# Softmax sums of an attention block: four buffers of P, other blocks summed by GpSimd, query and key roundings on ScalarE

## The reference

```python
def attention(x, Wq, bq, Wk, bk, Wv, bv, Wp, bp):
    q, k, v = heads(x @ Wq + bq), heads(x @ Wk + bk), heads(x @ Wv + bv)
    att = jnp.einsum('bhtd,bhsd->bhts', q, k) * (1.0 / math.sqrt(D))
    # mask: causal, and every fourth key (s % 4 == 3) is left out
    att = jax.nn.softmax(jnp.where(mask == 0, -jnp.inf, att), axis=-1)
    y = jnp.einsum('bhts,bhsd->bhtd', att, v)
    return merge_heads(y) @ Wp + bp

x = x + _layernorm(attention(_layernorm(x), ...))
idx = jnp.argmax(jax.nn.log_softmax(logits) - jnp.log(-jnp.log(u)))
x = x + _layernorm(_layernorm(x) @ W[idx] + b[idx])
```

## Time and profile before

| | |
|---|---|
| median of 3 runs | 2435.17 us (2433.01 to 2436.12) |
| the profiled execution | 2434.55 us |
| its span, first to last instruction | 2432.6 us |
| mean granted TensorE clock | 0.987 of full speed |
| busy: PE / ACT / DVE / POOL | 2321.4 / 1719.4 / 1686.6 / 1408.3 us |

### The profile page before, as it was taken

One profiled execution on the slowest core, in us unless ns is written; L12 is line 12 of the kernel. 1 busy time (PEld: TensorE's weight loads), 2 busy tenths in 40 slices (PEclk: granted clock), 3 DMA queues, 4 the chain that ended last, 5 costly groups with the idle time before them and its releaser, 6 DMA issues.

```text
span 2432.6 us, 43804 instructions
## 1 busy us (share of the span) xinstructions
PE 2321.4 (95%) x15380; PEld 966.1 (40%) x15380; DVE 1686.6 (69%) x4832; ACT 1719.4 (71%) x3142; POOL 1408.3 (58%) x1318
## 2 busy tenths in 40 slices
PE   4899999999999999999999999999899999999996
PEld 2444443433454443433344443343334444334322
DVE  7867677676477678677466867777728676777774
ACT  6667676777777667677776867767767676776673
POOL 2245465685655457477854637657765455665734
PEclk9899999999999999999999999999999999999998
DMA  7213131121233113022132313102114231301001
GB/s 197 67 42 93 28 78 35 41 55 41 50 89 78 57 43 80 17 51 51 33 87 59 92 31 75 48 23 58 38 46 94 60 80 31 83 22 40 30 1 35
DMA packets 224357, 137.50 MB, mean 57 GB/s; under 512 B 146730, under 2 KB 196618, under 8 KB 224138
## 3 DMA queue, kind: packets, MB, share of 16 engines
q1 hardware_dynamic: 222310, 134.65, 22.1%
q10 hardware_dynamic: 1828, 0.07, 0.1%
HBM read 39.69 MB, written 16.78 MB: 23 GB/s over the span
## 4 chain that ended last, share of the span: by engine, by line
PE 74%; DVE 10%; ACT 6%; issue 5%; POOL 5%; DMA 1%; SPq 0%; POOLq 0%; ACTq 0%; DVEq 0%
PE acc L1303 13%; PE acc L1267 12%; PE acc L1287 11%; PE acc L1238 9%; PE acc L1239 9%; PE acc L1240 9%; PE acc L1318 8%; ACT P L949 4%; POOL P L817 3%; DVE acc L1042 2%; PE acc L1291 2%; DVE MP L1046 2%; DVE MHL L1057 1%; PE acc L1243 1%; DVE STA L1015 1%
## 5 line engine op out<-in xcount | busy, mean ns | idle before, releaser
L949 ACT ACTIVATE P<-acc,EX 128x512 f32<-128x512 f32 (+2 forms) x1920 | 1073.1, 641 | 314.5 <-PE acc L1291 153.9
L1046 DVE TENSOR_REDUCE MP<-acc 128x1 f32<-128x512 f32 (+1 forms) x1088 | 720.6, 679 | 254.2 <-PE acc L1267 250.7
L817 POOL TENSOR_TENSOR P<-P 128x512 f32<-128x512 f32 x546 | 682.3, 1280 | 84.1 <-PE acc L1303 48.8
L1267 PE MATMUL acc<-KST,QST 96*128 96x512 f16 (+10 forms) x2112 | 593.2, 334 | 27.5 <-DVE MP L1046 11.9
L1042 DVE CUSTOM_DVE_ANT_0 acc<-acc,CB 128x96 f32<-128x96 f32 (+7 forms) x1024 | 449.5, 455 | 211.3 <-PE acc L1267 207.7
L1287 PE MATMUL acc<-QST,KST 98*128 98x512 f16 (+2 forms) x1920 | 579.1, 355 | 16.6 <-DVE MP L1046 5.7
L1303 PE MATMUL acc<-P,V 128*32 128x512 f32 (+2 forms) x3840 | 443.1, 546 | 3.6 <-ACT P L949 2.9
L1267 PEld LDWEIGHTS acc<-KST,QST 96*128 96x128 f16 x2112 | 194.9, 98 | 335.9 <-issue 60.2
L1287 PEld LDWEIGHTS acc<-QST,KST 98*128 98x128 f16 x1920 | 182.9, 98 | 294.7 <-issue 71.5
L1318 PE MATMUL acc<-P,ONES 128*32 128x512 f32 (+2 forms) x2688 | 285.1, 517 | 2.0 <-ACT P L949 1.9
L796 POOL TENSOR_TENSOR RR<-RR,NHALF 128x1 f32<-128x1 f32 x256 | 141.9, 557 | 236.8 <-DVE NM L1020 236.0
(11 more groups left out here) (144 smaller groups left out, 2983.8 us busy)
## 6 DMA issues: line engine op xcount, KB each, us to landing
QST<-QKH SPq DMA_DIRECT2D x128, 128.0 KB, 3.2
XR<-in_L_attn_x_dram SPq DMA_DIRECT2D x60, 256.0 KB, 2.8
out_dram<-XR SPq DMA_DIRECT2D x60, 256.0 KB, 2.1
KST<-QKH SPq DMA_DIRECT2D x128, 96.0 KB, 2.7
XB<-in_L_attn_x_dram SPq DMA_DIRECT2D x48, 252.0 KB
QST<-QKL SPq DMA_DIRECT2D x64, 128.0 KB, 3.3
KST<-QKL SPq DMA_DIRECT2D x64, 96.0 KB, 2.7
XB<-in_L_attn_x_dram SPq DMA_DIRECT2D x20, 256.0 KB, 3.3
```

The lines of the kernel that those rows point to most:

```text
L817: e.tensor_tensor(P[:, acc, a, :], P[:, acc, a, :], P[:, buf, a, :], ALU.add).then_inc(g_s, 1)
L949: e.activation(P[:, p_buf[u, g, sb_], a, t0:512], bank(*step)[:, t0:512], ACT.Exp, scale=EX[:, 1:2]).then_inc(a_e, 1)
L1046: e.tensor_reduce(maxima(u, g)[:, r, a, ci:ci + 1], bank(*s)[:, 0:n], AX.X, ALU.max).then_inc(v_m, 1)
L1267: i = e.matmul(bank(*s)[:, 0:n], QST[0:96, h, 128 * r:128 * r + 128], KST[0:96, h, c0:c0 + n], start=True, stop=True)
```

## The change

- `on_pe`: of the whole blocks below the diagonal TensorE sums the last j - 1 (j > 0) instead of every block with sb % 3 == 1. Sums go from 1, 2, 3 of the whole blocks at j = 1, 2, 3 to 0, 1, 2; GpSimd adds blocks 1 to 2, 1 to 4 and 1 to 6 to block 0.
- P has four buffers. Block 0's is kept through its group; the other blocks take turns in three.
- V has 12 blocks of rows instead of 15: each unit j has its own three in every batch, and at a new batch waits for the last unit of the batch before. YX has three rows that turn over all units (the very last uses XR). Constants and biases that lay in V and YX move.
- "high" is a ScalarE copy (semaphore `a_h`) instead of a VectorE one.
- The planner makes plans with four windows, six each, instead of one with up to six, and takes the shortest.

```diff
 def on_pe(j, sb):
-    return sb >= 3 * j or sb % 3 == 1
+    return sb >= 3 * j - max(j - 1, 0)
...
     buf, first, before, held = {}, {}, {}, {}
-    last, acc = 2, 0
+    ring = [0, 1, 2, 3]
     for u in range(NB * NJ):
         for g in range(4):
-            new = [i for i in range(3) if i not in (acc, last)][0]
-            ring = [last, acc]
-            acc = first[u, g] = new
             for sb in range(3 * (u % NJ) + 3):
-                last = acc if sb == 0 else ring[(sb - 1) % 2]
-                buf[u, g, sb] = last
-                if last in held:
-                    before[u, g, sb] = held[last]
-                held[last] = u, g, sb
+                now = buf[u, g, sb] = ring.pop(0)
+                if sb:
+                    ring.append(now)
+                else:
+                    first[u, g] = now
+                if now in held:
+                    before[u, g, sb] = held[now]
+                held[now] = u, g, sb
+            ring.append(first[u, g])
...
-    ROUNDS, WINDOW = 5, 20000
+    ROUNDS, WINDOWS = 6, (20000, 30000, 45000, 60000)
...
-        self.rank = {key: step[0] for key, step in self.steps.items()}
-        plans = [self.run()]
-        for _ in range(self.ROUNDS):
-            self.rank = self.backwards()
-            if self.rank is None:
-                break
-            plans.append(self.run())
+        plans = []
+        for window in self.WINDOWS:
+            self.rank = {key: step[0] for key, step in self.steps.items()}
+            for _ in range(self.ROUNDS):
+                plans.append(self.run())
+                self.rank = self.backwards(window)
+                if self.rank is None:
+                    break
...
-                add("dve", at, 400 if which == "k" else 470, ("high", job), [("act", "evac", job)], [("QKH", ("sp", "spread", job))])
-                add("gp", at, 870 if which == "k" else 1110, ("rest", job), [("dve", "high", job)])
+                add("act", at, 420 if which == "k" else 540, ("high", job), [("act", "evac", job)], [("QKH", ("sp", "spread", job))])
+                add("gp", at, 870 if which == "k" else 1110, ("rest", job), [("act", "high", job)])
...
-        V = sb("V", [128, 3 * (NJ + 1), 512], F32)
+        V = sb("V", [128, 3 * NJ, 512], F32)
...
-        P = sb("P", [128, 3, 4, 512], F32)
+        P = sb("P", [128, 4, 4, 512], F32)
...
-        YX = sb("YX", [128, 4, 512], F32)
+        YX = sb("YX", [128, 3, 512], F32)
...
-                        if u > 1:
-                            ac.wait_ge(p_pv, PE["pv", u - 2, 3, 3 * ((u - 2) % NJ) + 2])
-                        e.activation(V[:, 3 * (u % (NJ + 1)) + i, :], ps, ACT.Copy, scale=CO[:, 2:3]).then_inc(a_v, 1)
+                        if u >= NJ:
+                            ac.wait_ge(p_pv, PE["pv", u // NJ * NJ - 1, 3, 3 * (u % NJ) + 2])
+                        e.activation(V[:, 3 * (u % NJ) + i, :], ps, ACT.Copy, scale=CO[:, 2:3]).then_inc(a_v, 1)
                     elif name == "p":
-                        if u:
-                            ac.wait_ge(g_r, GP["add_y", u - 1, i])
-                        e.activation(YX[:, i, :], ps, ACT.Copy, scale=CO[:, 3:4]).then_inc(a_y, 1)
+                        n = 4 * u + i
+                        if n == 4 * NU - 1:
+                            ac.wait_ge(d_o[0], 16 * len(range(0, 4 * NU - 4, 3)))
+                        elif n > 2:
+                            ac.wait_ge(g_r, GP["add_y", *divmod(n - 3, 4)])
+                        e.activation(yx(u, i), ps, ACT.Copy, scale=CO[:, 3:4]).then_inc(a_y, 1)
...
+                elif kind == "high":
+                    job = s[1]
+                    at, n = q_slot[job], 384 if job[0] == "k" else 512
+                    ac.wait_ge(a_q, AC["evac", job])
+                    if at > 1:
+                        was, wu, wm = q_job[at - 2]
+                        ac.wait_ge(d_qk[was][wm], 48 * (wu + 1))
+                    e.activation(QKH[:, at % 2, 0:n], SC[:, 2, 0:n], ACT.Copy).then_inc(a_h, 1)
...
-                    e.tensor_copy(QKH[:, at % 2, 0:n], SC[:, 2, 0:n]).then_inc(v_q, 1)
```

## The result

The changed kernel took 2453.98 us (median of 7 runs, 2445.29 to 2464.64), the kernel before 2433.62 in the same job: a ratio of 1.008 [1.0058, 1.0103]. It is slower; the forecast was 2395. The profiled execution of the changed kernel took 2463.51 us, near the top of its seven times. The page: span, busy time by engine, the chain by engine and by line.

What follows compares the result with a forecast made beforehand. TensorE's own instructions, busy 95% of the span, were taken as the bound. Sums -41.3, adds +8, buffers -10, roundings 0, lock +3, storage and plan 0 give -40.3: 2435.2 to 2395 us, range 2355 to 2442.

Steps and rivals of the forecast that it cites:

- TensorE's sums: Units with j > 0: 48 summing steps of 0.86 us leave TensorE, all taken as path, -41.3 us.
- The adds on GpSimd: Those blocks become 192 more adds, some 240 us on GpSimd, mostly hidden by order and buffers; taken at +8 us.
- Exponentials' waits for adds: Sign on ScalarE: under 20 us if the forecast is right, over 50 us if GpSimd is the bound.
- Rival A: GpSimd becomes the bound at j = 3, price 53 us instead of 8: 2447 us, slower; chance 0.11.
- Buffers and banks: Fourth P buffer and later opened sum bank remove most of ScalarE's waits; taken -10 us, bounds 0 and -28.7.
- storage: Waits for V rows and the three YX rows: price 0, with +5 us as the upper end.
- The roundings: 128 casts move from VectorE to ScalarE, 71 to 81 us more there; taken 0, bounds -17.6 and +20 us.
- The lock: GpSimd's add runs hold up VectorE's rounding of negated peaks, and TensorE behind it; taken +3 us, bounds -12 and +40.
- Rival B: Longer gapless GpSimd runs catch the peaks' step in 12 later groups of j = 3: 2448 us; chance 0.07.
- the small step summing over 80 us: Sign on VectorE that longer GpSimd runs decide: the rounding of the negated peaks, 42.2 us over 64, sums to over 80.
- The plan: New planner windows change every engine's order; taken 0, 48 us either way, named as what would most easily make it wrong.

Runs made afterwards that it cites:

- after: The changed kernel itself, with every part of the change: 2453.98 us, ratio 1.008 to the kernel before in the same job.
- a_oldsums: The changed kernel with the old choice of blocks for TensorE's sums (546 adds on GpSimd): 2470.35 us, ratio 1.014.
- a_psum: The changed kernel with the group's maxima reduced into PSUM, where the two small steps read them right after the last peak: 2353.11 us, ratio 0.9641.
- a_dvehigh_psum: The changed kernel with maxima in PSUM and the roundings back on VectorE, with its own plan: 2368.52 us, ratio 0.9712.
- before: The kernel without the change: 2433.62 us in the same job as the changed kernel.
- b_psum: The kernel before the change with the group's maxima reduced into PSUM and the two small steps following at once: 2412.18 us, ratio 0.9898.
- lock_age: Small kernel without the reference's work: runs of 32 GpSimd adds from a standstill, one VectorE scaling asked after add n; waits 1.15 us at 14, 19.44 at 16.
- a_dvehigh: The changed kernel with the roundings of query and key rows back on VectorE, planned so: 2412.62 us, ratio 0.9893.
- lock_alone: Small kernel without the reference's work: runs of 24 GpSimd adds, one small step of varied kind asked after the second add; a cast waited 27.00 us.

## Why the prediction was wrong

**TensorE's sums: right.** -41.3 us was to leave TensorE; its busy time fell by 40.2, at a lower granted clock. **The adds on GpSimd: right in size.** The sums and adds together were to give -41.3 + 8 = -33.3; the runs with the small steps off the port give -36. At j = 3 GpSimd is busy 165.99 us of a unit of 229 and 165.41 of one of 205, the 166 forecast. The windows of after, two units of j = 3, beside 1021.00 and 1609.00 in the earlier trace rows:

```profile
1039.00:1268.00 229.00, 210.11 (x1319) 81.51 (x1317) 149.35 (x340) 161.38 (x287) 165.99 (x147) 0.96 0.16 42
1637.00:1842.00 205.00, 194.46 (x1259) 77.41 (x1260) 137.73 (x312) 157.35 (x282) 165.41 (x147) 0.98 0.16 44
```

They were to be 3.4 us shorter; they are 17 and 2 us longer, with TensorE busy about 4 us more in the first although it has less to do, and not busy for 19 us. Exponentials' waits for adds stayed under the 20 us named (17.1). Rival A did not come.

**Buffers and banks: near in size, not shown in cause.** The two waits that the fourth buffer was to remove for the most part, 11.3 + 17.4 us in the earlier trace rows, are 17.1 + 1.9 in after. The wait for the sums fell by the choice of blocks, not by the buffer: with four buffers and the old choice, a_oldsums keeps it.

```profile
ACT P L968 <- PE acc L1329: 15.6, 11, 3.1
...
ACT P L968 <- POOL P L825: 0.2, 1, 0.2
```

There the buffer removes the wait for adds, and the new choice brings that back. -8 us, the remainder above, stands for buffers, storage and windows together where -10 + 0 was taken.

**The roundings: the size of the work right, their worth depends on the shut-out.** 41.0 + 33.8 = 74.8 us went to ScalarE, within the 71 to 81 forecast. With the small steps off the port the move gains 15 us (taken 0, bounds -17.6 and +20), part of it perhaps because the casts no longer meet the shut-out. With them on it, the move loses 22 (plan held) to 41 us. The bound of -17.6 left out a row: TensorE also waited 9.1 us for line 1042's peaks, more than the 5.7 counted. The Trainium skill (ScalarE: Activation LUTs, Rules for kernel authors) gives simple operations such as `add` and `mul` to VectorE and not to ScalarE; taken as a rule for this cast too, it agrees with after as it stands, and not with the kernels whose small steps are off the port, where a_psum is 15 us under a_dvehigh_psum.

**The lock: this is the step that failed.** It was taken at +3 with bounds of -12 and +40. The shut-out costs some 100 us in after and 26 in before: +75, by the ratios +82. Terms as measured, -36 - 15 - 8 + 75 = +16, against 2453.98 less 2435.17 = +18.8; as -8 is a remainder, that the sum closes says only that the jobs agree. Rival B, at 2448, named the mechanism and the place (12 of the 15 long waits are in units of j = 3, as it said), and had the least chance of all; its sign, the small step summing over 80 us, is there with 132.0. That its number is so near is in part luck: the lock was 19 us larger than its 56, the other terms 16 us better. Three readings were short:

- What it cost before was put at 12 us, from the wait at 1705.84 and one other row. The runs give 26. What lies between is not in the rows read; the short waits (the two small steps take 68.4 us in before and 22.2 in b_psum, and only 19.8 of the 68.4 are in long waits) and the lowered clock behind each stall, as read at 1153 us in after, are two candidates.
- The bound of +40 was half of twelve waits like the worst of before, 5.66 us of TensorE's time each, and some. The earlier trace rows show the wait as 7.12 us beside a run of 8 adds; in the trace it came at the 19th instruction of a run of 25, and what counts is what is left of a run once it has grown old. In after both the number of long waits (5 to 15) and what each waits (up to 14.32 us) grew.
- "All 64 together are now caught for 31 us" was held against rival B. Only 7 of the 64 came at the 11th instruction of a run or later; the 57 others say nothing of what an old run costs.

The reason that the prediction gave, longer runs by more adds, is at most a part: line 1068 sums to 101.9 us with the adds of before (a_oldsums). The fourth buffer, the new plan and the moved roundings are in that kernel too; the roundings alone, put into before's plan, leave it at 45.9 us. No run separates the buffer from the plan.

The Trainium skill (SBUF — State Buffer, Who interferes with whom) lets the loser wait for one whole instruction. By that rule the term was 0. The runs do not agree: one instruction is what a request pays in a young run (1.15 us at 14 adds in lock_age), the rest of the run what it pays in an old one (19.44 us at 16). On who contends, the runs agree with that section: the reduction (0.20 us) and the step with its one tensor operand in PSUM (0.17) are untouched.

**The forecast's order of doubt.** The plan was named as what would most easily make it wrong; with after's plan held, the roundings' move was still worth 22 us of the 41. So the plan was about half of that difference; its share in the whole change no run shows. In the kernels with the small steps off the port the terms of the sum hold to within 15 us each: forecast without the lock's +3 -43, measured -59.

**Open.** Why a run grows old at all is not known, nor why at the 11th instruction at the latest in after and only past the 15th in lock_age, nor whether every kind of GpSimd instruction counts alike. Three small steps of after did get in within 1 us at the 14th to 19th instruction of a run, each during or just before line 804 or the run's end; whether any short instruction lets VectorE in, or this one alone, was not tried. How much of the 41 us of a_dvehigh is its order was held apart only from one side.

## What to carry to other kernels

Work moved to an engine is priced not only by that engine's own slack but by whom its longer runs shut out: look for a small step on the path whose greatest duration is many times its least, and ask what grows it. If GpSimd runs without a gap beside VectorE, take VectorE's small steps on the path off the shared port (here by an operand in PSUM, 2454 to 2353 us), or let GpSimd stand still for a moment every eight adds (2372), and not at every one (2451). A part undone by itself can mislead: the roundings lost 22 to 41 us with the shut-out in place and gained 15 with the small steps off the port.

## What the runs showed of the hardware

- In lock_age VectorE's step on the shared port waits for about one add (1.14 to 1.15 us) up to 14 adds after GpSimd last stood still, and for the rest of the run from 16 on: 19.44 us at 16 of 32 adds of 512 columns, 10.80 us at 16 with 256 columns. In lock_alone a cast waited 27.00 us. In after the first long wait, 12.30 us, came at the 11th instruction of a run.
- A GpSimd power step of one column ends such a wait without a standstill: 12 of the 15 long waits of after ended within 0.14 us after the start of one.
- A standstill as short as a wait for the engine's own last add opens the port: with it before every add the step takes 1.27 us in lock_alone.
- Waiting for its own last add at every eighth add left GpSimd 13.5 us of idle time; at all 546 adds of before it cost the kernel 17.6 us.
- Behind a stall of 13.65 us TensorE was granted 0.50 of its clock over 1153 to 1158 us and 0.93 over the 5 us after that.
